# Seven tiles of gathered rows fetched one row at a time by SyncE, in a graph message-passing kernel

## The chip, the cores and the metric

The kernel runs on one core of a Trainium2 chip. The metric is device time in microseconds (us) from start to end of one execution; lower is better. Engines are called PE (TensorE), DVE (VectorE), ACT (ScalarE), POOL (GpSimd) and SP (SyncE). SP only issues DMA transfers.

## The reference

The inputs are 6,250 nodes with 96 features, and 106,250 edges sorted by destination, each with 96 features of its own.

```python
h = jnp.maximum(_layernorm(x, axis=-1), 0.0)
ea = edge_attr @ W_edge.T + b_edge
msg = jax.nn.relu(h[src] + ea)                       # one row per edge
aggr = jax.ops.segment_sum(msg, dst, num_segments=6250)
z = (1.0 + eps) * h + aggr
out = x + jax.nn.relu(z @ W1.T + b1) @ W2.T + b2
```

## The kernel before

**Stages.** First h = relu(layernorm(x)) is computed and stored in DRAM as `h_table`. Then the edges are handled in tiles of 128 edges. There are 830 tiles and a tail of 10 edges, and the tiles are grouped in 43 batches: forty of 20 tiles, then batches of 16, 10 and 4. At the end a two-layer MLP runs over ten blocks of nodes.

**A batch of 20 tiles.** SP loads the transposed edge features with four transfers (`load_edges`, L320). POOL gathers the 128 source rows of each tile from `h_table` with one indirect DMA per tile (`gather`, L375), so a batch costs POOL 20 such instructions; the row numbers are in `src_all`, one column for each tile. PE multiplies the edge features by `w_edge` (L505; it writes them by feature). ACT moves 32x32 blocks out of PSUM (`move_blocks`, L451). DVE transposes them back (L926) and adds the gathered rows in two instructions of ten tiles each (`add_rows`, L941). ACT and DVE split the sum in three bf16 parts (L458, L920, L463, L955). PE sums the parts by destination with a one-hot matrix (L567, L604), which DVE adds up (L853, L825) before it makes the next one-hot matrix (L771).

**What sets the order.** Each engine has a list of its own, and semaphores tie the lists. `edge_in` and `gathered` have two buffers each (`SLOTS = 2`).

- POOL starts the gathers of batch c when PE has begun the edge product of batch c-1 (`edge_begun`) and DVE has added batch c-2 (`added`).
- SP starts the loads of batch c when PE has finished the edge product of batch c-2 (`edge_done`). In batches 17 to 26 it also issues two transfers that fetch x again (L356).
- ACT moves the blocks of batch c when `edge_done` counts c+1.
- On PE the sums of batch c-1 (`agg_done`) stand ahead of the edge product of batch c+1.
- On DVE the adds of batch c stand ahead of the sums of batch c-1.

Of the kernel before, what the change touches and what calls it, by code (L numbers as in the profile page):

```python
# [7 lines left out]
ALU = mybir.AluOpType  # L8
# [8 lines left out]
SIDES = 2  # L17
# [4 lines left out]
BANK = 512  # L22
LN_EPS = 1e-5
LAST_SIDES = (8, 5, 2)
SLOTS = 2
NODE_PARTS = 125
NODE_RUN = 5
# [28 lines left out]
    return [SIDE_TILES] * (rest // (SIDES * SIDE_TILES)) + list(LAST_SIDES)  # L56


def gnn_layer(nc, x, edge_t, src_tiles, dst_tiles, dst_rows, w_edge_t, b_edge,
              eps, w1_t, b1, w2_t, b2, out):  # L60
    N, D = x.shape
    E = edge_t.shape[1]
# [16 lines left out]
    def used_by(c, p, ring):  # L79

        return next((b for b in range(c - ring, -1, -ring) if p < len(pairs[b])), None)

    gathers_to = [[sum(groups[b][g][1] - groups[b][g][0] for b in range(c % SLOTS, c + 1, SLOTS) if g < len(groups[b]))
                   for g in range(len(groups[c]))] for c in range(BATCHES)]
    loads_to = [[sum(g < len(groups[b]) for b in range(c % SLOTS, c + 1, SLOTS)) for g in range(len(groups[c]))]
                for c in range(BATCHES)]
# [29 lines left out]
    with ExitStack() as ctx:  # L116
        def sb(name, shape, dt=F32):
            return ctx.enter_context(nc.sbuf_tensor(name, shape, dt))
# [41 lines left out]
        edge_blocks = sb("edge_blocks", [128, MOST * D])  # L160
        edge_tail_in = sb("edge_tail_in", [D + 1, TAIL])
        tail_gathered = sb("tail_gathered", [TAIL, D])

        dst_by_row = sb("dst_by_row", [BOUND_ROWS, dst_rows.shape[1]], I32)

# [35 lines left out]
        edges_in = [[sem(f"edges_in{b}{g}") for g in range(GROUPS)] for b in range(SLOTS)]  # L201
        gather_in = [[sem(f"gather_in{b}{g}") for g in range(GROUPS)] for b in range(SLOTS)]
        tail_in = sem("tail_in")
        tail_gather_in = sem("tail_gather_in")
        tail_edge_done = sem("tail_edge_done")
        tail_added = sem("tail_added")
# [66 lines left out]
        def flat_rows(rows, k0, k1):  # L273
            if k1 - k0 == PAIR_TILES:
                return rows[:, k0 * D:k1 * D].rearrange("e (h c) -> e h c", h=2)
            return rows[:, k0 * D:k1 * D]

        def in_rows(rows, k0, k1):
            if k1 - k0 == PAIR_TILES:
                return rows[:, k0 * D:k1 * D].rearrange("e (h t d) -> e h t d", h=2, d=D)  # L280
            return rows[:, k0 * D:k1 * D].rearrange("e (t d) -> e t d", d=D)
# [27 lines left out]
        @block.sync  # L309
        def _(sp):  # L310
            sp.dma_start(src_all[:, 0:tiles_of[0]], src_tiles[:, 0:tiles_of[0]]).then_inc(src_first_in, 16)
            for c in range(LN_CHUNKS):
                for a, b in spread:
                    sp.dma_start(x_all[a:b, chunk_of(c)], x_dram[a:b, chunk_of(c)]).then_inc(x_in[c], 16)
            sp.dma_start(w_edge[0:D, :], w_edge_t).then_inc(weights_in, 16)
            sp.dma_start(w_edge[D:D + 1, :], b_edge.rearrange("(a d) -> a d", a=1)).then_inc(weights_in, 16)

            def load_edges(c):
                for g, (k0, k1) in enumerate(groups[c]):
                    sp.dma_start(edge_in[c % SLOTS][0:D, k0 * EDGE_TILE:k1 * EDGE_TILE],  # L320
                                 edges_of(c, k0, k1 - k0)).then_inc(edges_in[c % SLOTS][g], 16)
# [12 lines left out]
            sp.dma_start(src_all[:, tiles_of[0]:TILES + 1], src_tiles[:, tiles_of[0]:TILES + 1]).then_inc(src_rest_in, 16)  # L334
            for c in range(1, len(TABLE_PARTS)):
                if c != ACT_PARTS - 1:
                    store_table(c)
            sp.wait_ge(table_stored, 16 * len(spread) * len(TABLE_PARTS))
            sp.dma_start(dst_by_row[:], dst_rows).then_inc(dst_rows_in, 16)
            sp.dma_start(dst_all[:], dst_tiles).then_inc(dst_in, 16)  # L340
            sp.dma_start(edge_tail_in[0:D, :], edge_t[:, TILES * EDGE_TILE:E]).then_inc(tail_in, 16)
            load_edges(1)
            sp.dma_start(scale_eps[:], eps.rearrange("(a b) -> a b", a=1).broadcast_to((D, 1))).then_inc(late_weights_in, 16)
            sp.dma_start(w1[:], w1_t).then_inc(late_weights_in, 16)
            sp.dma_start(b1_col[:], b1.rearrange("(d a) -> d a", a=1)).then_inc(late_weights_in, 16)
            sp.dma_start(w2[0:D, 0:D], w2_t).then_inc(late_weights_in, 16)
            sp.dma_start(w2[D:D + 1, 0:D], b2.rearrange("(a d) -> a d", a=1)).then_inc(late_weights_in, 16)

            for c in range(SLOTS, BATCHES):
                sp.wait_ge(edge_done, c - SLOTS + 1)  # L350
                load_edges(c)
                if X_FROM <= c < X_FROM + BLOCKS:
                    sp.wait_ge(table_stored, 16 * len(spread) * len(TABLE_PARTS))
                    sp.wait_ge(base_put, BASES)
                    for a, b in spread:
                        sp.dma_start(x_blocks[a:b, c - X_FROM, :], x_by_block[a:b, c - X_FROM, :]).then_inc(x_again_in, 16)  # L356

            for c in range(BLOCKS):
                sp.wait_ge(result_done, c + 1)
                for a, b in spread:  # L360
                    sp.dma_start(out_dram[a:b, c, :], x_blocks[a:b, c, :]).then_inc(stored, 16)
            sp.wait_ge(stored, 16 * BLOCKS * len(spread))

        @block.gpsimd
        def _(pool):
            nc.gpsimd.memset(ident[:], 0.0).then_inc(ident_made, 1)
            pool.wait_ge(ident_made, 1)
            nc.gpsimd.affine_select(out=ident[:], in_=ident[:], compare_op=ALU.not_equal, fill=1.0, base=0,
                                    pattern=[[-1, 128]], channel_multiplier=1).then_inc(ident_made, 1)
            nc.gpsimd.iota(iota_sb[:], [[1, WINDOW]], base=0, channel_multiplier=0,  # L370
                           allow_small_or_imprecise_dtypes=True).then_inc(iota_made, 1)
            def gather(table, c, k):
                at = k * D
                tile = first_tile[c] + k
                nc.gpsimd.indirect_dma_start(  # L375
                    out=gathered[c % SLOTS][:, at:at + D], out_offset=None, in_=table,
                    in_offset=bass.IndirectOffsetOnAxis(ap=src_all[:, tile:tile + 1], axis=0),
                ).then_inc(gather_in[c % SLOTS][k // GROUP_TILES], 16)

            pool.wait_ge(src_first_in, 16)  # L380
            for k in range(FIRST_BURST):
                gather(x, 0, k)
            pool.wait_ge(norm_ready, len(LN_PARTS))
            for k in range(FIRST_BURST, tiles_of[0]):
                gather(x, 0, k)
            pool.wait_ge(src_rest_in, 16)
            pool.wait_ge(table_stored, 16 * len(spread) * len(TABLE_PARTS))
            nc.gpsimd.indirect_dma_start(
                out=tail_gathered[:], out_offset=None, in_=h_table,
                in_offset=bass.IndirectOffsetOnAxis(ap=src_all[0:TAIL, TILES:TILES + 1], axis=0),  # L390
            ).then_inc(tail_gather_in, 16)
            for c in range(1, BATCHES):
                if c >= SLOTS:
                    pool.wait_ge(edge_begun, c)
                for p, (k0, k1) in enumerate(pairs[c]):
                    last_use = used_by(c, p, SLOTS)
                    if last_use is not None:
                        pool.wait_ge(added, adds_to[last_use] + p + 1)
                    for k in range(k0, k1):
                        gather(h_table, c, k)  # L400

        @block.scalar
# [269 lines left out]
        def _(dve):  # L672
# [256 lines left out]
            def add_rows(c):  # L929
                slot = c % SLOTS  # L930
                if by_feature(c):
                    dve.wait_ge(edges_turned, turned_to[c + 1])
                else:
                    dve.wait_ge(edge_done, c + 1)
                for p, (k0, k1) in enumerate(pairs[c]):
                    for g, (g0, g1) in enumerate(groups[c]):
                        if k0 <= g0 < k1:
                            dve.wait_ge(gather_in[slot][g], 16 * gathers_to[c][g])
                    for a, b in pieces(c, k0, k1):
                        put = in_banks(c, a, b) if c < LATE else in_rows(gathered[slot], a, b)  # L940
                        last = nc.vector.tensor_tensor(put, in_banks(c, a, b), in_rows(gathered[slot], a, b), ALU.add)  # L941
                    last.then_inc(added, 1)

            def take_high(c):
# [98 lines left out]
```

## Time and profile before

| | us |
|---|---|
| median of 3 runs | 1229.39 (1229.15 to 1229.55) |
| the profiled execution | 1224.89 |
| span in that execution, first to last instruction | 1223.1 |
| POOL busy | 785.8 |
| DVE busy | 607.6 |
| ACT busy | 518.7 |
| PE busy | 496.0 |

The span is the time between the first and the last instruction; 1.8 us of the profiled execution lie around it. Busy time counts the instructions of an engine and leaves out waits, register work and the issuing of DMAs by SP. An engine that is busy for much less than the span can still set the pace, if its instructions stand apart for a fixed time.

### The profile page before, as it was taken

How to read it: one execution, taken by the hardware profiler on the slowest of the kernel's cores; microseconds unless marked ns; L12 is line 12 of the kernel's file. 1: busy time of each engine (PE TensorE's matmuls, PEld its weight loads, DVE VectorE, ACT ScalarE, POOL GpSimd, SP SyncE). 2: the span in 40 equal slices, each digit the busy share in tenths (PEclk: the TensorE clock that was granted, in tenths of full speed). 3: DMA queues.
4: the chain of work that ended last, by engine and by line, in shares of the span. 5: the costliest groups of instructions: out<-in, count | busy, mean ns of one | idle time of the engine just before them, and what ended most of it. 6: DMA issues, size and time to landing. Idle time of an engine off the chain costs nothing.

```text
span 1223.1 us, 7306 instructions
## 1 busy us (share of the span) xinstructions
PE 496.0 (41%) x1592; PEld 249.7 (20%) x1592; DVE 607.6 (50%) x739; ACT 518.7 (42%) x713; POOL 785.8 (64%) x838
## 2 busy tenths in 40 slices
PE   2143344344344334245343253442534334425358
PEld 2011111222121112012111121120211111112146
DVE  6665544555554445364536345352545363543563
ACT  5134444344433335353435333343535343433434
POOL 6766666666666666575757575766757575757530
PEclk9967766767767766566666665666656666666669
DMA  7523333222223223242323332322423232322212
GB/s 217 148 66 71 83 78 68 67 68 68 67 67 68 68 68 98 56 112 71 81 71 80 72 79 64 72 68 61 101 54 82 63 72 64 71 64 67 47 28 79
DMA packets 51178, 93.18 MB, mean 76 GB/s; under 512 B 17722, under 2 KB 20443, under 8 KB 51136
## 3 DMA queue, kind: packets, MB, share of 16 engines
q0 software_dynamic: 26592, 40.85, 16.1%
q1 hardware_dynamic: 24390, 51.63, 15.6%
q8 instruction: 14, 0.23, 0.1%
q10 hardware_dynamic: 154, 0.24, 0.1%
q14 instruction: 28, 0.23, 0.1%
HBM read 87.85 MB, written 4.80 MB: 76 GB/s over the span
## 4 chain that ended last, share of the span: by engine, by line
another core or an unknown queue 32%; ACT 23%; issue 21%; DVE 13%; PE 6%; DVEq 4%; DMA 1%; SPq 0%; ACTq 0%
ACT edge_blocks L451 17%; ACT msg_parts L458 3%; DVE turn_ps L941 3%; DVE turn_ps L920 3%; PE turn_ps L505 2%; DVEq L834 2%; DVE turn_ps L926 2%; ACT msg_parts L463 2%; DVE msg_parts L955 1%; PE agg_ps L604 1%; PE turn_ps L667 1%; DVEq L836 1%; DVE stats L705 1%; DVE acc L825 1%
## 5 line engine op out<-in xcount | busy, mean ns | idle before, releaser
L375 POOL DMA_INDIRECT gathered<-h_table,src_all x810 | 764.4, 944 | 382.0 <-issue 237.7
L451 ACT COPY edge_blocks<-turn_ps 32x640 f32<-32x640 f32 (+1 forms) x480 | 325.9, 679 | 475.9 <-remote 358.8
L505 PE MATMUL turn_ps<-edge_in,w_edge 97*96 97x512 f32 x398 | 268.2, 842 | 324.2 <-issue 258.8
L926 DVE STREAM_TRANSPOSE turn_ps<-edge_blocks 128x960 f32<-128x960 f32 (+1 forms) x81 | 89.7, 1153 | 216.4 <-ACT edge_blocks L451 115.8
L853 DVE TENSOR_REDUCE sums<-agg_ps 128x192 f32<-128x576 f32 x41 | 30.9, 753 | 319.8 <-remote 319.8
L505 PEld LDWEIGHTS turn_ps<-edge_in,w_edge 97*96 97x96 f32 x398 | 88.6, 234 | 482.9 <-issue 482.9
L604 PE MATMUL agg_ps<-msg_parts,select 128*128 128x288 bf16 x816 | 155.6, 367 | 0.0
L458 ACT ACTIVATE msg_parts<-turn_ps 128x960 bf16<-128x960 f32 (+1 forms) x83 | 79.2, 957 | 157.2 <-DVE turn_ps L941 110.3
L771 DVE TENSOR_TENSOR select<-const_ps,dst_rel 128x2560 bf16<-128x2560 f32 (+1 forms) x43 | 120.8, 2812 | 33.2 <-issue 28.5
L604 PEld LDWEIGHTS agg_ps<-msg_parts,select 128*128 128x128 bf16 x816 | 103.4, 127 | 46.1
L941 DVE TENSOR_TENSOR turn_ps<-turn_ps,gathered 128x960 f32<-128x960 f32 (+1 forms) x83 | 91.1, 1144 | 2.1 <-DVE gathered L760 0.5
L920 DVE SCALAR_TENSOR_TENSOR turn_ps<-turn_ps,msg_parts 128x960 f32<-128x960 f32 (+1 forms) x83 | 91.1, 1144 | 0.3 <-ACT msg_parts L458 0.3
L955 DVE TENSOR_TENSOR msg_parts<-turn_ps,msg_parts 128x960 bf16<-128x960 f32 (+1 forms) x83 | 90.8, 1136 | 0.3 <-ACT msg_parts L463 0.3
L552 PE MATMUL turn_ps<-ident,h_all 125*96 125x125 f32 x50 | 13.1, 415 | 188.4 <-ACT edge_blocks L451 179.9
L567 PE MATMUL agg_ps<-ident,sums 128*96 128x128 f32 x84 | 23.6, 378 | 150.5 <-DVE acc L825 133.9
L463 ACT CAST msg_parts<-turn_ps 128x960 bf16<-128x960 f32 (+1 forms) x83 | 78.2, 945 | 11.6 <-issue 6.6
L552 PEld LDWEIGHTS turn_ps<-ident,h_all 125*96 125x96 f32 x50 | 7.9, 187 | 199.3 <-issue 199.2
L567 PEld LDWEIGHTS agg_ps<-ident,sums 128*96 128x96 f32 x84 | 10.3, 162 | 174.4 <-issue 171.7
L375 POOL DMA_INDIRECT gathered<-x_dram,src_all x20 | 19.6, 981 | 10.9 <-issue 5.5
L526 PE MATMUL turn_ps<-w_edge,edge_in 97*128 97x96 f32 x68 | 14.4, 406 | 27.1 <-DMA edge_in<-edge_t_dram 14.9
L825 DVE TENSOR_TENSOR acc<-acc,agg_ps 96x128 f32 x84 | 23.4, 279 | 0.9
L526 PEld LDWEIGHTS turn_ps<-w_edge,edge_in 97*128 97x128 f32 x68 | 13.9, 315 | 27.3 <-issue 27.3
(77 smaller groups left out, 187.9 us busy)
## 6 DMA issues: line engine op xcount, KB each, us to landing
edge_in<-edge_t_dram SPq DMA_DIRECT2D x165, 240.0 KB
gathered<-h_table,src_all POOLq DMA_INDIRECT x810
x_all<-x_dram SPq DMA_DIRECT2D x5, 420.0 KB
h_all<-x_dram SPq DMA_DIRECT2D x10, 210.0 KB
out_dram<-h_all SPq DMA_DIRECT2D x10, 210.0 KB
h_table<-h_all SPq DMA_DIRECT2D x3, 420.0 KB
h_table<-h_all SPq DMA_DIRECT2D x1, 630.0 KB
dst_by_row<-dst_rows_dram SPq DMA_DIRECT2D x1, 480.0 KB, 4.1
```

What stands on the lines that cost most here:

```text
L375: nc.gpsimd.indirect_dma_start(out=gathered[c % SLOTS][:, at:at + D], out_offset=None, in_=table, in_offset=bass.IndirectOffsetOnAxis(ap=s ...
L451: last = nc.scalar.copy(blocks[e:e + TURN, :, f:f + TURN], edges[f:f + TURN, :, e:e + TURN])
L458: last = nc.scalar.activation(in_parts(msg_parts[c % 2], a, b, 0), in_banks(c, a, b), ACT.Relu)
L463: last = nc.scalar.copy(in_parts(msg_parts[c % 2], a, b, 1), in_banks(c, a, b))
L505: mm = pe.matmul(turn_ps[0:D, q * BANK:q * BANK + (k1 - k0) * EDGE_TILE], w_edge[:], edge_in[c % SLOTS][:, k0 * EDGE_TILE:k1 * EDGE_TILE], ...
L604: mm = pe.matmul(agg_ps[:, s * BANK:s * BANK + SPLIT * D], select[c % 2][:, tile, :], msg_parts[c % 2][:, tile, :, :], start=(t == 0), sto ...
L771: nc.vector.tensor_tensor(select[b][:, 0:tiles, :], iota_ps.unsqueeze(1).broadcast_to((128, tiles, WINDOW)), dst_rel[:, bass.ds(at, tiles) ...
L825: return nc.vector.tensor_tensor(acc[:, cols], acc[:, cols], turned, ALU.add)
L920: return nc.vector.scalar_tensor_tensor(message, message, 0.0, high, ALU.max, ALU.subtract)
L926: last = nc.vector.transpose(in_flat(c, a, b), flat_rows(edge_blocks, a, b))
L941: last = nc.vector.tensor_tensor(put, in_banks(c, a, b), in_rows(gathered[slot], a, b), ALU.add)
L955: last = nc.vector.tensor_tensor(in_parts(msg_parts[c % 2], a, b, 2), in_banks(c, a, b), in_parts(msg_parts[c % 2], a, b, 1), ALU.subtract)
```

## The change

In seven of the forty large batches (6, 11, 16, 21, 26, 31 and 36) POOL gathers 19 tiles and leaves out the last. The 128 rows of that tile are fetched by SP, with one transfer of one row (384 bytes) each, into a buffer of their own (`row_tile`, two of them). The row numbers lie in one partition (`row_index`). SP loads up to 16 of them in registers with one load, and takes the address of each transfer in `h_table` from a register. The 128 transfers of a tile are spread over five batches (25 or 26 in each), after the edge loads of that batch in SP's list: batches 2 to 6 for the first tile, and so on, up to batch 36. Ahead of the first rows of the third and each later tile, SP waits for the adds of the batch that last used the same buffer. DVE adds the second ten tiles of such a batch in three instructions (five tiles, four tiles, and the last tile after a wait for its 128 transfers).

```diff
+ROW_STEPS = 5
+ROW_SLOTS = 2
+PICK = 16
+def row_plan(tiles):
+    plan = batch_plan(tiles)
+    full = plan.index(LAST_SIDES[0])
+    return list(range(SLOTS + ROW_STEPS - 1, full, ROW_STEPS))
...
+    POOL_TILES = [n - (c in row_tile_of) for c, n in enumerate(tiles_of)]
...
+            sp.dma_start(row_index[:], row_src).then_inc(row_index_in, 16)
+            picked = [sp.alloc_register(f"sp_row{i}") for i in range(PICK)]
+            def load_rows(c):
+                j, step = divmod(c - SLOTS, ROW_STEPS)
+                if j >= ROWED:
+                    return
+                if c == SLOTS:
+                    sp.wait_ge(row_index_in, 16)
+                if step == 0 and j >= ROW_SLOTS:
+                    sp.wait_ge(added, adds_to[rowed[j - ROW_SLOTS] + 1])
+                k0, k1 = (EDGE_TILE * n // ROW_STEPS for n in (step, step + 1))
+                for k in range(k0, k1):
+                    if (k - k0) % PICK == 0:
+                        count = min(PICK, k1 - k)
+                        at = j * EDGE_TILE + k
+                        sp.load(picked[0:count], row_index[0:1, at:at + count])
+                    node = sp.snap(picked[(k - k0) % PICK], min_val=0, max_val=N - 1)
+                    sp.dma_start(row_tile[j % ROW_SLOTS][k:k + 1, :],
+                                 h_table[bass.ds(node, 1), :]).then_inc(rows_in[j % ROW_SLOTS], 16)
             for c in range(SLOTS, BATCHES):
                 sp.wait_ge(edge_done, c - SLOTS + 1)
                 load_edges(c)
...
+                load_rows(c)
...
-                    for k in range(k0, k1):
+                    for k in range(k0, min(k1, POOL_TILES[c])):
                         gather(h_table, c, k)
...
+                    if k1 > POOL_TILES[c]:
+                        j = row_tile_of[c]
+                        in_bank = groups[c][-1][0]
+                        for a, b in ((k0, in_bank), (in_bank, POOL_TILES[c])):
+                            nc.vector.tensor_tensor(in_part(c, a, b), in_part(c, a, b), gathered[slot][:, a * D:b * D], ALU.add)
+                        dve.wait_ge(rows_in[j % ROW_SLOTS], 16 * EDGE_TILE * (j // ROW_SLOTS + 1))
+                        own = in_part(c, POOL_TILES[c], k1)
+                        last = nc.vector.tensor_tensor(own, own, row_tile[j % ROW_SLOTS][:], ALU.add)
+                    else:
+                        for a, b in pieces(c, k0, k1):
...
```

## Rows read from the trace of the kernel before

**Rows 1.** The page, busy time of each engine with its share of the span.

```profile
PE 496.0 (41%) x1592; PEld 249.7 (20%) x1592; DVE 607.6 (50%) x739; ACT 518.7 (42%) x713; POOL 785.8 (64%) x838
```

**Rows 2.** Table of waits: total us, times, longest.

```profile
ACT edge_blocks L451 <- remote: 358.8, 25, 17.7
...
POOL gathered L375 <- remote: 138.0, 26, 6.9
```

**Rows 3.** The page, groups by cost: busy us, mean ns, idle before and what ended it.

```profile
L375 POOL DMA_INDIRECT gathered<-h_table,src_all x810 | 764.4, 944 | 382.0 <-issue 237.7
```

**Rows 4.** Timeline of POOL, 404 to 434 us: start, us, instruction, idle before.

```profile
404.68 0.94 POOL L375 DMA_INDIRECT gathered<-h_table,src_all  x1 [3.75 <-remote]
...
428.40 0.94 POOL L375 DMA_INDIRECT gathered<-h_table,src_all  x1 [0.30 <-issue]
433.02 0.94 POOL L375 DMA_INDIRECT gathered<-h_table,src_all  x1 [3.69 <-remote]
```

**Rows 5.** Timeline of POOL, 742 to 802 us.

```profile
743.97 0.94 POOL L375 DMA_INDIRECT gathered<-h_table,src_all  x1 [6.88 <-remote]
...
792.64 0.95 POOL L375 DMA_INDIRECT gathered<-h_table,src_all  x1 [0.30 <-issue]
800.47 0.94 POOL L375 DMA_INDIRECT gathered<-h_table,src_all  x1 [6.88 <-remote]
```

**Rows 6.** Timeline of all engines, stretch 760 to 801 us.

```profile
768.12 8.31 ACT L451 COPY edge_blocks<-turn_ps 32x640 f32<-32x640 f32 x12 [8.24 <-PE turn_ps L505]
...
778.75 2.23 DVE L941 TENSOR_TENSOR turn_ps<-turn_ps,gathered 128x960 f32<-128x960 f32 x2
...
783.14 2.22 DVE L955 TENSOR_TENSOR msg_parts<-turn_ps,msg_parts 128x960 bf16<-128x960 f32 x2
...
784.44 7.74 PE L505 MATMUL turn_ps<-edge_in,w_edge 97*96 97x512 f32 x10 [13.69 <-issue]
...
800.19 0.76 DVE L853 TENSOR_REDUCE sums<-agg_ps 128x192 f32<-128x576 f32 x1 [14.83 <-remote]
```

**Rows 7.** Busy time by window: PE, PEld, DVE, ACT, POOL, PEclk, DMA share, GB/s.

```profile
431.00:432.60 1.60, 0.00 (x0) 0.00 (x0) 0.00 (x0) 0.00 (x0) 0.00 (x0) 0.50 0.00 0
```

**Rows 8.** Timeline of POOL, first gathers after four other stops.

```profile
517.92 0.94 POOL L375 DMA_INDIRECT gathered<-h_table,src_all  x1 [6.86 <-remote]
...
574.47 0.94 POOL L375 DMA_INDIRECT gathered<-h_table,src_all  x1 [6.94 <-remote]
...
1139.46 0.94 POOL L375 DMA_INDIRECT gathered<-h_table,src_all  x1 [6.88 <-remote]
...
1177.03 0.94 POOL L375 DMA_INDIRECT gathered<-h_table,src_all  x1 [5.40 <-PE turn_ps L526]
```

**Rows 9.** Instructions of L356: count, shortest/median/longest ns, first and last start.

```profile
L356 SPq DMA_DIRECT2D h_all<-x_dram x20: 8/402/708, 463.1 to 715.6; - x20
```

**Rows 10.** Timeline of SP, first 40 us and one batch at 461 us.

```profile
5.84 0.28 SPq L316 DMA_DIRECT2D w_edge<-b_edge_dram  x1
6.17 1.80 SPq L320 DMA_DIRECT2D edge_in<-edge_t_dram  x4
...
14.39 0.76 SPq L334 DMA_DIRECT2D src_all<-src_tiles_dram  x1
...
461.28 1.72 SPq L320 DMA_DIRECT2D edge_in<-edge_t_dram  x4
```

**Rows 11.** Register work on DVE (L834, L866, L828): shortest/median/longest ns.

```profile
L834 DVEq TENSOR_LOAD <-bounds_i x86: 298/303/547, 71.3 to 1183.5; - x86
...
L866 DVEq FUSED_REGOPS  x39: 62/63/70, 93.9 to 1158.4; - x39
...
L828 DVEq FUSED_REGOPS  x86: 231/254/268, 93.1 to 1194.7; - x86
```

**Rows 12.** The page, DMA queues: packets, MB, share of 16 engines.

```profile
q0 software_dynamic: 26592, 40.85, 16.1%
```

**Rows 13.** Groups by shape, DVE: busy us, mean ns, idle before.

```profile
L941 DVE TENSOR_TENSOR turn_ps<-turn_ps,gathered 128x960 f32<-128x960 f32 x81 | 90.4, 1161 | 2.1 <-DVE gathered L760 0.5
```

More of the change, by code:

```diff
@@ L56, in batch_plan, with gnn_layer @@
     return [SIDE_TILES] * (rest // (SIDES * SIDE_TILES)) + list(LAST_SIDES)
-def gnn_layer(nc, x, edge_t, src_tiles, dst_tiles, dst_rows, w_edge_t, b_edge,
+def row_plan(tiles):
+    plan = batch_plan(tiles)
+    full = plan.index(LAST_SIDES[0])
+    return list(range(SLOTS + ROW_STEPS - 1, full, ROW_STEPS))
+def gnn_layer(nc, x, edge_t, src_tiles, row_src, dst_tiles, dst_rows, w_edge_t, b_edge,
               eps, w1_t, b1, w2_t, b2, out):
@@ L81, in used_by @@
         return next((b for b in range(c - ring, -1, -ring) if p < len(pairs[b])), None)
-    gathers_to = [[sum(groups[b][g][1] - groups[b][g][0] for b in range(c % SLOTS, c + 1, SLOTS) if g < len(groups[b]))
+    rowed = row_plan(TILES)
+    ROWED = len(rowed)
+    row_tile_of = {c: j for j, c in enumerate(rowed)}
+    POOL_TILES = [n - (c in row_tile_of) for c, n in enumerate(tiles_of)]
+    gathers_to = [[sum(min(groups[b][g][1], POOL_TILES[b]) - groups[b][g][0]
+                       for b in range(c % SLOTS, c + 1, SLOTS) if g < len(groups[b]))
                    for g in range(len(groups[c]))] for c in range(BATCHES)]
@@ L162, in gnn_layer @@
         tail_gathered = sb("tail_gathered", [TAIL, D])
+        row_index = sb("row_index", [1, ROWED * EDGE_TILE], I32)
+        row_tile = [sb(f"row_tile{b}", [EDGE_TILE, D]) for b in range(ROW_SLOTS)]
         dst_by_row = sb("dst_by_row", [BOUND_ROWS, dst_rows.shape[1]], I32)
@@ L203, in gnn_layer @@
         tail_in = sem("tail_in")
+        row_index_in = sem("row_index_in")
+        rows_in = [sem(f"rows_in{b}") for b in range(ROW_SLOTS)]
         tail_gather_in = sem("tail_gather_in")
@@ L276, in flat_rows, with in_part @@
             return rows[:, k0 * D:k1 * D]
+        def in_part(c, k0, k1):
+            g = k0 // GROUP_TILES
+            at = k0 % GROUP_TILES * D
+            return edge_bank(c, g)[:, at:at + (k1 - k0) * D]
         def in_rows(rows, k0, k1):
@@ L938, in add_rows @@
                             dve.wait_ge(gather_in[slot][g], 16 * gathers_to[c][g])
-                    for a, b in pieces(c, k0, k1):
-                        put = in_banks(c, a, b) if c < LATE else in_rows(gathered[slot], a, b)
-                        last = nc.vector.tensor_tensor(put, in_banks(c, a, b), in_rows(gathered[slot], a, b), ALU.add)
+                    if k1 > POOL_TILES[c]:
[8 more added lines that the diff above has]
+                        for a, b in pieces(c, k0, k1):
+                            put = in_banks(c, a, b) if c < LATE else in_rows(gathered[slot], a, b)
+                            last = nc.vector.tensor_tensor(put, in_banks(c, a, b), in_rows(gathered[slot], a, b), ALU.add)
                     last.then_inc(added, 1)
@@ L1013, in by_tile, with by_row @@
         return np.pad(index, (0, tiles * EDGE_TILE - E)).reshape(tiles, EDGE_TILE).T
+    def by_row(index):
+        plan_of = [SIDES * m for m in plan]
+        tiles = [sum(plan_of[:c + 1]) - 1 for c in row_plan(E // EDGE_TILE)]
+        return np.concatenate([index[t * EDGE_TILE:(t + 1) * EDGE_TILE] for t in tiles]).reshape(1, -1)
     def by_side(index):
@@ L1022 @@
         "src_tiles": by_tile(src),
+        "row_src": by_row(src),
         "dst_tiles": by_tile(dst),
```

## The prediction

> **What bounds the kernel now.** I read the page first: no engine is busy for more than 64% of the span, and POOL is the one with 64% [rows 1]. So the question is not which engine is full but who waits for whom. The table of waits says that ACT stood 358.8 us at its block moves and POOL 138.0 us at its gathers, both put down to "remote", a releaser that the profile doesn't know [rows 2]. The groups by cost show that POOL's 810 gathers took 764.4 us, with 237.7 us more in small gaps where nothing was awaited [rows 3]: a gather is 0.94 us and stands 1.25 us from the next.
>
> The timeline of POOL shows how these go together. From about 100 to 490 us POOL runs 20 gathers, stops, and runs 20 more. Such a run starts at 404.68, its last gather at 428.40 (19 steps of 1.248 us), and the next run starts at 433.02: 28.34 us for 20 gathers [rows 4]. After 517 us the runs have 40 gathers: 743.97 to 800.47, 56.50 us [rows 5]. The stop is not a constant: POOL stands 3.69 us after 20 gathers and 6.88 after 40. The difference of the two runs is 28.16 us for 20 gathers, **1.408 us for one**, and only 0.18 us is left over that doesn't grow with the count. So the stop behaves like a backlog of 0.16 us per gather that has to be worked off before PE's signals get through.
>
> Is it really POOL's side, and not the chain of PE, ACT and DVE? One turn of the chain is seen from 768.12: block moves 8.31 us, DVE's adds at 778.75, the last split ends at 785.36, and PE's edge product ends at 784.44 + 7.74 = 792.18 [rows 6]. That is 24.1 us, and the turn before it was released at once. Then DVE, which waits for PE's sums, stands 14.83 us until 800.19, although PE's last recorded product ended 8.0 us earlier. In the shorter runs the same hole shows no instruction on any engine and no DMA at all [rows 7]. What holds PE's signals there I can't name from the profile. But its length goes with the number of gathers in three kinds of run, and two turns of the chain need 48.2 us where the pair takes 56.5. I take it that the middle part, from 40 to 1177 us, costs 1.408 us per gather and hides some 4 us per batch of everything else.
>
> **The change, part by part.** *POOL.* Seven gathers go, one in each of seven batches: 7 x 1.408 = **9.9 us less**. If only the visible step counts, it is 7 x 1.248 = 8.7; if the pace were the chain's, 0. The last run before the end has 26 gathers and takes 37.57 us, 1139.46 to 1177.03 [rows 8], 0.8 more than 28.34 + 6 x 1.408 = 36.8, so the rate holds to 2% there too. I take 1.408. The Trainium skill (Perfetto Trace Analysis, on GPSIMD instructions) says that a GpSimd span is to be timed by start-to-start spacing, not by its duration. By that rule alone the sum would be 8.7 us; the stops say 9.9.
>
> *Does SP's extra traffic load the same hidden thing?* Only a look at other extra transfers can tell. In ten batches SP issues two more transfers (L356, 463.1 to 715.6 us) [rows 9]. The pair of batches from 517.92 to 574.47 has them and takes 56.55 us [rows 8]; the pair from 743.97 has none and takes 56.50. Four more transfers for 0.05 us: 0.01 us each at most. There are 896 row transfers, so that bound is wide: 0 to 11 us back. Four large transfers carried much more data than 51 single rows, so I take 0 and keep 11.
>
> *SP.* A batch gets 25.6 rows on average. One transfer of one row of 384 bytes stands in the trace: it starts at 5.84 and the next at 6.17, 0.33 us. Its address is fixed; the slowest single issue near it took 0.76 (L334) [rows 10]. The register work of a row is not in the trace for SP. On DVE a fused register step takes 0.063 us (one bounded value) to 0.254 (a handful of operations), and a register load 0.303 [rows 11]. So a row costs 0.33 + 0.06 = 0.4 at least and 0.8 + 0.25 + 0.3 = 1.35 at most; I take 0.33 + 0.25 = 0.6, nearest to the like-sized transfer. Per batch that is 25.6 x 0.6 = 15.4, two loads 0.7, and the four edge loads 1.7: 17.8 us. SP has 27 to 28 us per batch and otherwise sleeps, so nothing is late: the next `edge_done` finds it free. The point at which it would not is (27.5 - 2.4) / 25.6 = 0.98 us per row. SP's own new wait (for `added` of a batch five or more back) is long met when SP gets to it. The load of `row_index` is one issue of about 0.4 us at the start, before a stretch in which SP waits.
>
> *DVE.* One add of 1.161 us becomes three shorter ones [rows 13]. Three cost at most 3 x 1.161, 2.3 us more, hidden in the 4 us that the chain has spare per batch; more likely 0.3. Without that cover it would be 2 us over seven batches. The wait for the rows: the last fifth is issued after `edge_done` of two batches earlier, some 50 us before the add, so it passes.
>
> *Gathers themselves.* All row transfers may end up on few DMA engines. The Trainium skill (DMA: Bandwidth & Descriptors, on why a DMA increments its semaphore by 16) says that a one-row transfer runs on one engine, the lowest-numbered. Worked out from the trace: POOL's queue moved 26592 packets in 16.1% of 16 engines' span, 0.118 us per packet [rows 12]. If 26 rows a batch sit on one engine at twice that, it is 6 us of 28. Gathers land at least 7 us before their add (a run's half ends at 768.9, its rows are added at 778.75 or later), so this is hidden.
>
> **Sum.** On the profiled execution 1224.89 - 9.9 = 1215.0. The median of the runs is 4.5 above that execution, so **1219.5**.
>
> **Rivals.**
>
> 1. *The rows load what holds PE's signals* (chance 0.13). For it: that thing is unnamed, and 896 more transfers are many beside 830 gathers. Against: L356 left no trace. At 0.006 us per row half the gain goes (1224.5); at 0.011 all of it (1229.4).
> 2. *SP becomes the bound* (0.19, slower). The mechanism: issuing a row with a register address takes over 0.98 us; then SP's list for a batch outlasts POOL's 27.5 us, edge loads come later each time, and all 35 batches run at SP's pace. At 1.0 us per row this is 28.0 against 28.2, no change yet; at 1.1 it is 30.6, +2.4 x 35 = +84, so 1313; at 1.35 some 37, over 1500. For it: no row shows a register address on SP. Against: the plain issue costs a third of the limit.
> 3. *The pace is the chain's* (0.08). Then nothing changes: 1229.4. For it: the stops are ended by PE. Against: a stop twice as long after twice the gathers, and the 24.1 us turn.
> 4. *Rows crowd one DMA engine* (0.05, slower). It decides if a row holds its engine for over 0.8 us, since 25.6 of them then fill 20 us or more of a batch and gathers come later than the 7 us that they have. If each of the seven stretches of five batches loses 3 us by it, that is 21 - 9.9 = 11 more: about 1240.
>
> The forecast has 0.55: 1217 to 1222. A measurement of this kernel can tell about 0.2%, 2.5 us. Faster by more: forecast and the upper half of rival 1, 0.62. The same: the rest of rival 1, rival 3, a little of rival 2, 0.14. Slower: 0.24. The range reaches from 1217 to 1240; only an SP-bound run lies far above.
>
> **What would show it.** POOL: 803 gathers at 1.25 us spacing, and stops 1.4 us earlier in each run with a rowed batch (55.1 us for 39). SP: rows 0.4 to 0.8 us apart, and edge loads still right after `edge_done`. Wrong would be: edge loads that follow a row without a wait and runs stretched to SP's list (rival 2); unchanged run lengths of 28.3 and 56.5 (rival 3); longer stops after equally many gathers (rival 1); DVE waiting at L941 (rival 4).

## The result and the profile after

| | us |
|---|---|
| before, median of 4 runs beside it | 1229.47 (1229.15 to 1229.75) |
| after, median of 4 runs | 1467.18 (1465.09 to 1469.67) |
| ratio, 95% interval | 1.1934 (1.1913 to 1.1956) |
| after, the profiled execution and its span | 1468.46, 1466.7 |

The change costs 238 us. The forecast was 1219.5. Ratios here and below are of the undisturbed executions; the medians also include single executions that ran 2 to 15% longer than their fellows (1153.97 in e2, 1251.86 in g4, 1238.71 in the kernel before beside f1 to f3).

The page of the changed kernel gives the first answer in its busy times and in the chain that ended last. The columns of the first line are those of [rows 1].

```profile
PE 480.5 (33%) x1592; PEld 241.9 (16%) x1592; DVE 608.9 (42%) x753; ACT 518.9 (35%) x713; POOL 780.4 (53%) x831
...
SPq 52%; issue 39%; DVE 3%; PE 3%; ACT 2%; DMA 1%; DVEq 1%; ACTq 0%
SPq L391 28%; SPq L390 11%; SPq L389 7%; SPq L344 4%; ACT edge_blocks L497 1%; PE turn_ps L713 1%; DVE turn_ps L966 1%; DVE stats L751 1%; SPq L401 1%; PE turn_ps L551 0%; PE turn_ps L659 0%; DVEq L880 0%; PE agg_ps L696 0%; DMA h_table<-h_all 0%; ACT h_all L464 0%
```

No engine does notably more work than in [rows 1] (DVE 608.9 us against 607.6). Half of the chain is SP's own queue: the row transfers (L391), the register step ahead of each (L390), the register loads (L389) and the edge loads (L344). In the kernel before SP's queue was 0% of that chain. "Issue" (39%) stands between SP's instructions too, as the batch shown below will tell.

The table of waits of the changed kernel (total us, times, longest) shows what hangs on it.

```profile
PEld turn_ps L551 <- DMA edge_in<-edge_t_dram: 562.4, 67, 31.4
PE turn_ps L551 <- DMA edge_in<-edge_t_dram: 529.0, 25, 31.1
...
POOL gathered L421 <- PE turn_ps L551: 369.5, 33, 17.4
...
DVE turn_ps L992 <- DMA row_tile<-h_table: 106.6, 7, 18.7
```

PE waits 529.0 us for edge features, which SP loads. POOL then waits for PE's edge product (369.5 us; in [rows 2] its longest wait was 138.0 us, for a releaser the profile doesn't know), and DVE waits once in each of the seven batches for the row tile, 106.6 us in all.

The timeline of SP shows that its list is what fills a batch (start, us from the first to the last of the group, count).

```profile
99.34 1.73 SPq L344 DMA_DIRECT2D edge_in<-edge_t_dram  x4
...
524.26 1.73 SPq L344 DMA_DIRECT2D edge_in<-edge_t_dram  x4
527.41 30.16 SPq L391 DMA_DIRECT2D row_tile<-h_table  x26
557.62 1.73 SPq L344 DMA_DIRECT2D edge_in<-edge_t_dram  x4
...
1275.90 1.73 SPq L344 DMA_DIRECT2D edge_in<-edge_t_dram  x4
```

The 26 rows end at 557.57 and the next edge loads start at 557.62: SP never sleeps between 99 and 1312 us. From 99.34 to 1275.90 there are 33 batches, 35.7 us each, against 28.3 in [rows 4, 5].

How that comes to 238 us is read from PE, whose edge products of batches 3 and 36 start here (the kernel before first, then the changed one).

```profile
108.90 4.50 PE L505 MATMUL turn_ps<-edge_in,w_edge 97*96 97x512 f32 x10 [2.57 <-issue]
...
1042.65 6.64 PE L505 MATMUL turn_ps<-edge_in,w_edge 97*96 97x512 f32 x10 [9.55 <-issue]
```

```profile
114.79 4.50 PE L551 MATMUL turn_ps<-edge_in,w_edge 97*96 97x512 f32 x10 [2.76 <-issue]
...
1278.87 7.36 PE L551 MATMUL turn_ps<-edge_in,w_edge 97*96 97x512 f32 x10 [23.70 <-DMA edge_in<-edge_t_dram]
```

The 33 batches take 1164.1 us instead of 933.8: 230.3 more, 7.0 each. With 5.9 us ahead of batch 3 and 7.4 behind the start of batch 36 this is 243.6, the difference of the two profiled spans (1466.7 and 1223.1). In the kernel before the loads of batch 36 were issued at 993.7, 49 us ahead of the product that needs them; in the changed kernel at 1275.90, 3 us ahead.

Why do 26 rows take 30 us? The instructions of SP in two stretches of this one batch tell it. The first three lines are 527 to 540 us, the other three 540 to 556 (shortest/median/longest ns).

```profile
L390 SPq FUSED_REGOPS  x19: 3/44/712, 527.3 to 539.6; - x19
L391 SPq MOVE row_tile<-h_table x18: 3/29/29, 527.3 to 538.2; - x18
L391 SPq DMA_DIRECT2D row_tile<-h_table x18: 3/228/699, 527.4 to 538.2; - x18
...
L390 SPq FUSED_REGOPS  x5: 13/700/725, 539.6 to 553.7; - x5
L391 SPq MOVE row_tile<-h_table x5: 12/701/719, 540.3 to 555.1; - x5
L391 SPq DMA_DIRECT2D row_tile<-h_table x5: 697/710/1402, 540.3 to 555.8; - x5
```

In the first stretch 18 rows go out, 13 of them up to 532.9: 44 ns for the register step, 29 ns for a move and 228 ns for the transfer, 0.42 us from row to row.

```profile
L391 SPq DMA_DIRECT2D row_tile<-h_table x13: 148/228/406, 527.4 to 532.5; - x13
```

In the 16 us from 540 five rows go out. Each of the three instructions takes about 0.70 us there, even the 29 ns move, and there are gaps of 0.70 us between them as well, so that the rows stand 2.8 to 4.9 us apart. The last three rows, from 556.5, are fast again. The timeline of POOL and of DVE in the same stretch shows when this ends.

```profile
552.06 0.94 POOL L421 DMA_INDIRECT gathered<-h_table,src_all  x1 [0.30 <-issue]
562.98 0.94 POOL L421 DMA_INDIRECT gathered<-h_table,src_all  x1 [9.98 <-PE turn_ps L551]
```

```profile
556.57 0.76 DVE L899 TENSOR_REDUCE sums<-agg_ps 128x192 f32<-128x576 f32 x1 [4.32 <-remote]
```

POOL's gathers run from 529.58 to 553.0. At 556.57 DVE gets PE's signal, and SP's last slow instruction ends at 556.47. In the kernel before the stops end in the same way, with the signal to DVE (800.19 in [rows 6]) and POOL's next gather right behind it (800.47 in [rows 5]). I take it that what holds PE's signals in the kernel before is what slows SP's instructions in this one; the two times 0.1 us apart are the evidence, and no run shows the thing itself.

### The profile page after: what moved, and what is told of

It is laid out like the page before. It is cut to its first block, busy times and chain, and to the rows that moved or that the text cites. A ratio compares the mean times of both kernels' runs of the same rounds, so it can differ in the third digit from the quotient of the medians.

```text
span 1466.7 us, 10074 instructions
## 1 busy us (share of the span) xinstructions
PE 480.5 (33%) x1592; PEld 241.9 (16%) x1592; DVE 608.9 (42%) x753; ACT 518.9 (35%) x713; POOL 780.4 (53%) x831
## 4 chain that ended last, share of the span: by engine, by line
SPq 52%; issue 39%; DVE 3%; PE 3%; ACT 2%; DMA 1%; DVEq 1%; ACTq 0%
SPq L391 28%; SPq L390 11%; SPq L389 7%; SPq L344 4%; ACT edge_blocks L497 1%; PE turn_ps L713 1%; DVE turn_ps L966 1%; DVE stats L751 1%; SPq L401 1%; PE turn_ps L551 0%; PE turn_ps L659 0%; DVEq L880 0%; PE agg_ps L696 0%; DMA h_table<-h_all 0%; ACT h_all L464 0%
## 5 line engine op out<-in xcount | busy, mean ns | idle before, releaser
L421 POOL DMA_INDIRECT gathered<-h_table,src_all x803 | 759.0, 945 | 630.8 <-PE turn_ps L551 369.5
L551 PE MATMUL turn_ps<-edge_in,w_edge 97*96 97x512 f32 x398 | 283.8, 884 | 781.3 <-DMA edge_in<-edge_t_dram 529.0
L551 PEld LDWEIGHTS turn_ps<-edge_in,w_edge 97*96 97x96 f32 x398 | 93.1, 246 | 950.1 <-DMA edge_in<-edge_t_dram 562.4
L650 PE MATMUL agg_ps<-msg_parts,select 128*128 128x288 bf16 x816 | 128.9, 323 | 0.0
L650 PEld LDWEIGHTS agg_ps<-msg_parts,select 128*128 128x128 bf16 x816 | 90.8, 111 | 31.1
L996 DVE TENSOR_TENSOR turn_ps<-turn_ps,gathered 128x960 f32<-128x960 f32 (+1 forms) x76 | 83.7, 1143 | 2.0 <-DVE gathered L806 0.5
L598 PE MATMUL turn_ps<-ident,h_all 125*96 125x125 f32 x50 | 13.1, 415 | 116.2 <-ACT edge_blocks L497 65.2
L992 DVE TENSOR_TENSOR turn_ps<-turn_ps,row_tile 128x96 f32<-128x96 f32 x7 | 1.9, 266 | 106.6 <-DMA row_tile<-h_table 106.6
L613 PE MATMUL agg_ps<-ident,sums 128*96 128x128 f32 x84 | 20.1, 329 | 25.0 <-DVE acc L852 20.4
```

Of the source, the lines that this page charges most:

```text
L421: nc.gpsimd.indirect_dma_start(out=gathered[c % SLOTS][:, at:at + D], out_offset=None, in_=table, in_offset=bass.IndirectOffsetOnAxis(ap=s ...
L551: mm = pe.matmul(turn_ps[0:D, q * BANK:q * BANK + (k1 - k0) * EDGE_TILE], w_edge[:], edge_in[c % SLOTS][:, k0 * EDGE_TILE:k1 * EDGE_TILE], ...
L650: mm = pe.matmul(agg_ps[:, s * BANK:s * BANK + SPLIT * D], select[c % 2][:, tile, :], msg_parts[c % 2][:, tile, :, :], start=(t == 0), sto ...
```

## The experiments

The experiments gave two kinds of result, and without that no number below can be understood: in some groups of runs the kernel before takes about 1224 us and the traces have POOL's stops, in others it takes about 1080 and the traces have none. I write **S** for a chip with stops and **N** for one without. S were chips 4 (e5 to e7) and 11 (g), N were chips 2 (e1 to e4), 14 (f), 8 (h) and 3 (i). Each chip served one group of runs, so the record does not show whether the kind belongs to the chip or to something else that changed between groups. The clock does not make the difference: in the kernel before the mean granted clock was 0.67 to 0.69 on S and 0.69 to 0.71 on N. Every comparison is with the kernel before on the same chip. The first measurement (1229 us) is of kind S. Two theories stood: **A**, SP's list of instructions is longer than a batch, and **B**, the row transfers themselves slow the gathers or PE's signals.

**e1_pool_only.** POOL's part alone.

```diff
-                load_rows(c)
...
-                        dve.wait_ge(rows_in[j % ROW_SLOTS], 16 * EDGE_TILE * (j // ROW_SLOTS + 1))
...
+            for rows in row_tile:
+                nc.vector.memset(rows[:], 0.0)
```

> POOL's part alone: seven gathers fewer, no row is fetched, and DVE adds a tile of zeros for the seven tiles, without a wait (so these tiles' messages lack their source rows). If a gather costs 1.41 us with its share of the stops, 1219.5 us; if only its visible step of 1.25 us, 1220.7; if the chain of PE, ACT and DVE sets the pace, 1229.4. The loss of the changed kernel should be gone in every theory that puts it on SP or on the rows.

Kind N: 1071.33 against 1080.0, ratio 0.9922 (0.9907 to 0.9937), 8.7 us less = 7 x 1.24. The visible step of a gather counts there, and nothing more.

**e2_rows_only.** SP's part alone.

```diff
-                    for k in range(k0, min(k1, POOL_TILES[c])):
+                    for k in range(k0, k1):
```

> SP's part alone: all 896 rows are fetched and waited for, and POOL gathers all 20 tiles in every batch (the rows still come from the row tile). Theory A, SP's list of instructions is the bound: the changed kernel's 1467 us, give or take 15, since POOL's seven gathers are not on the path. Theory B, the row transfers slow down the gathers or PE's signals themselves: 1467 + 10 = 1477.

Kind N: 1081.29 against 1080.0, ratio 1.0009 (0.9999 to 1.0019). 896 rows by SP cost nothing that can be told from no change. Neither theory's number came, as both started from the loss of kind S.

**e3_ten_steps.** The rows of a tile over ten batches, three tiles.

```diff
-ROW_STEPS = 5
+ROW_STEPS = 10
```

> The same rows spread over ten batches each: three tiles, 12 or 13 rows per batch. Theory A, SP's list is the bound: 13 rows take one register load of about 2.8 us and 13 x 0.42 us, 10 us with the edge loads, which SP has behind it before its instructions slow down; SP waits for PE again and the time is 1229.4 - 3 x 1.41 = 1225.2. Theory B, each row transfer costs the rest a fixed time ((1467 - 1219.5) / 896 = 0.28 us): 384 rows give 1225.2 + 106 = 1331.

Kind N: 1075.73 against 1080.0, ratio 0.9965 (0.9953 to 0.9977), 4.3 us less. Three steps of 1.25 us are 3.7.

**e4_fixed_address.** The transfers without register work.

```diff
-                        sp.load(picked[0:count], row_index[0:1, at:at + count])
-                    node = sp.snap(picked[(k - k0) % PICK], min_val=0, max_val=N - 1)
+                    node = (j * EDGE_TILE + k) * 6 % N
...
-                                 h_table[bass.ds(node, 1), :]).then_inc(rows_in[j % ROW_SLOTS], 16)
+                                 h_table[node:node + 1, :]).then_inc(rows_in[j % ROW_SLOTS], 16)
```

> All 896 row transfers at addresses known when the program is built, so SP issues one instruction per row and not three, and loads no registers (the rows fetched are other nodes' rows). Theory A, the count of SP instructions at 0.70 us each is what overruns the batch: at most 26 x 0.7 + 1.7 = 20 us per batch, under POOL's 27, so about 1219.5. Theory B, the transfers themselves cost the time: 1467.

Kind N: 1072.16 against 1080.0, ratio 0.993 (0.9915 to 0.9945), like e1. On this kind it tells nothing about A and B. The four runs together show that there neither the rows nor the register work cost anything that can be told from no change, and POOL has no stops: in each of the four traces its gathers from `h_table` follow one another to the last, less than 1.9 us from start to start.

**e5_change_again.** The changed kernel, unaltered.

> The changed kernel itself, unaltered, beside the kernel before on the chip of these runs. The four runs so far had the kernel before at 1080 us and not at 1229, with no stops of POOL and every transfer's landing in the trace. Theory A in its new form: the stops and SP's slow instructions are one thing that belongs to the chip (or to its recording) of the first measurement; where it is missing the change gives 7 x 1.25 = 8.7 us, 1071. If it comes back here: 1229 before and 1467 after. Theory B, the change is slow by itself: some 240 us over the kernel before on this chip too, near 1320.

This chip was of kind S: 1446.42 against 1224.44, ratio 1.1821 (1.1794 to 1.1849). The loss comes back with the stops.

**e6_registers_only.** Meant as the register work without transfers.

```diff
-                    sp.dma_start(row_tile[j % ROW_SLOTS][k:k + 1, :],
-                                 h_table[bass.ds(node, 1), :]).then_inc(rows_in[j % ROW_SLOTS], 16)
+                    sp.reg_mov(kept, node)
...
```

> SP loads the 896 row numbers into registers and makes an address value of each, and issues no row transfer; a tile of zeros is added (the seven tiles lack their source rows). POOL as in the changed kernel. On a chip without the stops: 1071, like POOL's part alone. On a chip with them: SP has 2 short instructions per row and not 3 and no transfer; if it is the number of instructions that slows SP, the time falls to two thirds of the loss (some 1380); if it is the transfers, to 1219.5.

Kind S: 1215.09 against 1224.44, ratio 0.9924 (0.9909 to 0.9939), 9.4 us less. But the program has 7322 instructions, where the changed kernel has 10074: the register work, whose results nobody used, was removed when the kernel was compiled. So it says nothing on registers. It is POOL's part alone on kind S, and it gives 9.4 us for seven gathers; the forecast of this term was 9.9. The interval of the ratio, 7.5 to 11.1 us, would hold 8.7 as well. POOL's timeline decides: a run of 39 gathers starts here, then one of 40, then the next one of 39.

```profile
459.32 0.94 POOL L421 DMA_INDIRECT gathered<-h_table,src_all  x1 [3.82 <-remote]
...
514.41 0.94 POOL L421 DMA_INDIRECT gathered<-h_table,src_all  x1 [6.70 <-remote]
...
570.92 0.94 POOL L421 DMA_INDIRECT gathered<-h_table,src_all  x1 [6.88 <-remote]
```

The 39 take 55.09 us and the 40 take 56.51, and 55.1 for 39 was the prediction's sign. A gather costs 1.41 us there, stop included.

**e7_four_steps.** Nine tiles, each over four batches.

```diff
-ROW_STEPS = 5
+ROW_STEPS = 4
```

> Nine tiles by SP, each spread over four batches, so 32 rows per batch. On a chip without the stops SP needs 1.7 + 32 x (0.42 + 0.22) = 22 us of a batch of 25, so it still waits for PE, and the time is 1080 - 9 x 1.25 = 1068.8. On a chip with the stops SP's list is longer still: (32 / 25.6) times the changed kernel's 34.8 us per batch, 43 us in 36 batches, near 1750.

Kind S: 1529.19 against 1224.44, ratio 1.2482 (1.2465 to 1.2499). More rows per batch, more loss, but much less than in proportion to SP's list (1750 was expected). A reason may be that POOL stands idle for a longer part of each batch, so that more rows go out at the fast rate; no run tests it.

**f1_fixed_address** and **f2_ten_steps** (kernels as e4 and e3), and **f3_half_rows**, the kernel before with gathers of half the rows:

```diff
-                    out=gathered[c % SLOTS][:, at:at + D], out_offset=None, in_=table,
-                    in_offset=bass.IndirectOffsetOnAxis(ap=src_all[:, tile:tile + 1], axis=0),
+                    out=gathered[c % SLOTS][0:64, at:at + D], out_offset=None, in_=table,
+                    in_offset=bass.IndirectOffsetOnAxis(ap=src_all[0:64, tile:tile + 1], axis=0),
```

> The same kernel as in the run with fixed addresses before (896 row transfers, one SP instruction each, no register work; other nodes' rows are fetched), in the hope of a chip with the stops, where the kernel before takes 1225 to 1229. There: if three SP instructions per row at 0.70 us each are what overruns the batch, one instruction per row fits (20 us of 27) and the time is near 1219.5; if the row transfers themselves cost the time, it stays near 1450. Without the stops: 1072 again.

> Three tiles, 12 or 13 rows per batch, as before, for a chip with the stops. If SP's list is the bound only when it is longer than POOL's batch, 13 rows (10 us at SP's fast rate, at most 13 x 2.1 + 4.5 = 32 us at the slow one, mostly the fast one) leave SP free: 1225 - 3 x 1.41 = 1221. If each row costs a fixed time (0.28 us by the changed kernel), 1221 + 106 = 1327. Without the stops: 1075.7 again.

> The kernel before with gathers of 64 rows each (the first 64 edges of each tile; the other 64 get zeros), and as many gathers as before, no row by SP. It asks what the stops of POOL grow with. If with rows moved, the backlog per gather is half of 1.41 us and under the step, so the stops go, and the time falls to POOL's step times 810 or to the chain's 24 us per batch, 1060 or less. If with the count of gather instructions, the stops stay as they are: 1225. Without the stops on this chip it only gives POOL's step for 64 rows.

All three fell on kind N. f1: 1070.44 against 1080.37, ratio 0.9915 (0.99 to 0.993). f2: 1076.95, ratio 0.997 (0.9959 to 0.9981). f3: 1050.27, ratio 0.9722 (0.9707 to 0.9736), so that a gather of 64 rows costs nearly as much as one of 128. The profile has 903 ns instead of 944 and the same small gaps.

**g1_change, g2_fixed_address, g3_ten_steps, g4_half_rows.** The same four kernels, and this chip was of kind S (before: 1223.88).

> The changed kernel once more. Chips so far fall in two kinds: on three sets of runs the kernel before took 1224 to 1229 (twice) with stops of POOL, on two others 1080 without. On the first kind the change should give 1446 to 1467 again; on the second, where it has not run yet, 1080 - 8.7 = 1071.

1445.1, ratio 1.1789 (1.1727 to 1.1852). The loss is there for the third time.

> 896 row transfers with one SP instruction each and no register work. Of use on the kind of chip with stops: near 1219 if the count of SP instructions overruns the batch, near 1450 if the transfers do. On the other kind 1071 again.

1237.35, ratio 1.0113 (1.0052 to 1.0175). By e6's ratio POOL's part alone would be 1214.6 on this chip, so 896 transfers with one instruction each cost 23 us (16 to 31 by the interval of the ratio), and the changed kernel's cost 230. So it is not the transfers as such (B), but what SP has to get through for each. SP's table of waits shows that it sleeps again, where the changed kernel's waits at L344 came to 77 us (33 + 44), all of them after its last rows at 1312 us:

```profile
SPq L344 <- remote: 370.2, 24, 27.0
SPq L344 <- PE turn_ps L550: 68.2, 7, 22.5
```

> Three tiles by SP, 13 rows per batch. On the kind of chip with stops: 1221 if SP's list matters only where it is longer than POOL's batch, 1327 if each row costs a fixed time. On the other kind 1076 again.

1243.61, ratio 1.0168 (1.015 to 1.0186). It is between the two expected values: 24 us over the 1219.7 of three gathers fewer. The timeline of SP says why half the rows don't bring half the loss, nor none.

```profile
518.56 9.22 SPq L391 DMA_DIRECT2D row_tile<-h_table  x13
...
533.93 44.40 SPq L391 DMA_DIRECT2D row_tile<-h_table  x13
578.38 1.73 SPq L344 DMA_DIRECT2D edge_in<-edge_t_dram  x4
...
584.20 5.65 SPq L391 DMA_DIRECT2D row_tile<-h_table  x13
...
598.14 20.18 SPq L391 DMA_DIRECT2D row_tile<-h_table  x13
```

Thirteen rows take 5.7 us when they are issued in the fast part, and 44.4 us when they fall in the slow one; the edge loads that stand behind them are then late. The expectation that 13 rows would mostly meet the fast part was wrong.

> Gathers of 64 rows, as many as before, no rows by SP. On the kind of chip with stops: 1060 or less if the backlog grows with the rows or with time, 1225 if it grows with the number of gather instructions. On the other kind 1050 again.

1227.01, ratio 1.0024 (1.0012 to 1.0037). Half the rows, and the time (0.2% more) and the length of a run are as before: timeline of POOL, first gathers after two stops, to be read against [rows 5].

```profile
525.04 0.90 POOL L375 DMA_INDIRECT gathered<-h_table,src_all  x1 [8.38 <-remote]
...
581.52 0.91 POOL L375 DMA_INDIRECT gathered<-h_table,src_all  x1 [8.37 <-remote]
```

A run of 40 gathers takes 56.48 us (56.50 before), although each step is shorter; the stop makes up for it. So on kind S a gather instruction costs 1.41 us with its share of the stop, for 64 rows as for 128.

**h1_change, h2_registers_kept, h3_four_steps.** The change and e7 for kind N, and a kernel whose register work can't be removed:

```diff
-                    sp.dma_start(row_tile[j % ROW_SLOTS][k:k + 1, :],
-                                 h_table[bass.ds(node, 1), :]).then_inc(rows_in[j % ROW_SLOTS], 16)
+                    sp.reg_alu(kept, kept, node, ALU.max)
+                last_node = sp.snap(kept, min_val=0, max_val=N - 1)
+                sp.dma_start(kept_rows[j % ROW_SLOTS][step:step + 1, :],
+                             h_table[bass.ds(last_node, 1), :]).then_inc(rows_in[j % ROW_SLOTS], 16)
...
```

> The changed kernel, still without a time on the kind of chip where the kernel before takes 1080 us: there 1071. On the other kind 1445 again.

Kind N: **1070.96 against 1081.49, ratio 0.9913 (0.9895 to 0.9932)**. There the change is a gain, of 10.5 us. Its instructions of SP are all at the fast price (same columns as above), and its timeline shows SP asleep at the end of a batch:

```profile
L389 SPq TENSOR_LOAD <-row_index x70: 1016/2256/3572, 40.1 to 872.8; - x70
```

```profile
L390 SPq FUSED_REGOPS  x896: 44/44/59, 41.3 to 878.9; - x180
```

```profile
L391 SPq MOVE row_tile<-h_table x896: 29/29/37, 41.4 to 879.0; - x180
L391 SPq DMA_DIRECT2D row_tile<-h_table x896: 224/228/299, 41.5 to 879.1; - x180
```

```profile
488.99 1.73 SPq L344 DMA_DIRECT2D edge_in<-edge_t_dram  x4
...
495.43 13.17 SPq L391 DMA_DIRECT2D row_tile<-h_table  x26
515.17 1.73 SPq L344 DMA_DIRECT2D edge_in<-edge_t_dram  x4
```

The list of this batch ends at 508.6, 19.6 us after it began, and the next begins at 515.17. The slowest of 896 transfers took 299 ns; on the chip of the first measurement the slowest took 1412.

The same instructions, summed over all rowed batches in the two traces of the changed kernel, tell where the loss of kind S sits:

| SP, us in all | kind N (h1) | kind S (first measurement) |
|---|---|---|
| 70 register loads | 154 | 109 |
| 896 register steps | 40 | 163 |
| 896 moves | 26 | 140 |
| 896 transfers | 208 | 275 |
| gaps behind a step, a move or a transfer, up to the next one of these | 110 | 472 |

The loads do not take longer on kind S. The time is lost in the three short instructions of each row and in the gaps between them.

> SP loads all 896 row numbers into registers and takes the largest of them, and issues one transfer per batch with that address, not 25.6 (a tile of zeros is added for the seven tiles). It has the register loads of the changed kernel, the register steps packed into six per batch, and almost none of the transfers. On the kind of chip with stops: 1215, like POOL's part alone, if the row transfers and the many instructions between them fill SP's list; about 1215 + 35 x 3 = 1320 or more if the register loads (3.5 us for 16) alone were enough. On the other kind 1071.

Kind N: 1070.95, ratio 0.9911 (0.9892 to 0.993), as expected there. **i1_registers_kept** repeated it in the hope of kind S:

> The same kernel as in the run before with the registers kept (row numbers loaded, one transfer per batch). If this chip is of the kind with stops: 1215 if the register loads alone don't overrun SP's batch, 1320 or more if they do. Otherwise 1071 again.

Kind N again: 1074.26 against 1081.84, ratio 0.9924 (0.9908 to 0.9941); its profiled execution took 1084.05 at a granted clock of 0.59, the other four 1069.76 to 1074.67 at 0.70 to 0.71. No run has the loads without the rows on kind S; that they are not the loss is read from the sums above.

> Nine tiles by SP, 32 rows per batch. On the kind of chip without stops 1080 - 9 x 1.25 = 1068.8, a little better than the change, since SP's list of 22 us still fits in a batch of 25. On the other kind 1529 again.

Kind N: 1068.36, ratio 0.9887 (0.9869 to 0.9905), 13.1 us less for nine gathers. It is the fastest version with full gathers on kind N, and the slowest on kind S (e7). Its register loads are all cheap:

```profile
L389 SPq TENSOR_LOAD <-row_index x72: 1152/1227/1402, 40.6 to 894.8; - x72
```

Each of them loads 16 numbers and starts at a multiple of 16 bytes in `row_index`. In h1 only the loads of the first and fourth batch of each five start so: 28 of the 70, 1.0 to 1.4 us each. The other 42 took 3.5 to 3.6 us for 16 numbers and 2.1 to 2.4 for 9 or 10. e3's 30 loads of 12 or 13 numbers divide the same way, 0.9 to 1.3 us and 2.9 to 3.0.

**What tells the kinds apart in a trace.** The list of DMA issues ends with the median time from issue to landing. In the changed kernel's first profile it is missing, in the same kernel on kind N it is there:

```profile
edge_in<-edge_t_dram SPq DMA_DIRECT2D x165, 240.0 KB
```

```profile
edge_in<-edge_t_dram SPq DMA_DIRECT2D x165, 240.0 KB, 3.4
```

It is so in all the profiles: no landing time for these 165 transfers in the nine of kind S (before, after, e5, e6, e7 and g1 to g4), and one of 3.4 to 4.4 us in the profiles of kind N. Kind S loses records of semaphores: for the same 10074 instructions the trace of the changed kernel holds 6830 semaphore events in the first measurement and 19987 in h1. That would fit a recorder that can't keep up and makes the engines wait for it, since it is SP's cheapest instructions that take 0.70 us, and a gather costs 1.41 us, twice that, however little it moves. But every execution that gave a time has a span and a clock on record, so none is known to have run unrecorded; this was not tested, and the cause of the stops and of the slow instructions is not settled.

## Why the prediction was wrong

**The step that failed** is the price of a row on SP: "I take 0.33 + 0.25 = 0.6", from which "nothing is late". On kind N the sum was right: register step, move and transfer are 0.30 us of work and 0.42 us from row to row, and the loads, 22 us for a tile's ten in h1, add 0.17: 0.59 us per row. Part of that is luck, as the register step was taken too long (0.25 us for 0.04) and the loads too short (0.7 us for the two of a batch, where they took 2.2 to 5.9). On the chip of the measurement the same row costs 1.3 us on average, 35.7 us per batch instead of the 17.8 of the forecast for SP's list, because SP's short instructions take 0.70 us for most of a run of gathers.

**Where it should have been seen.** I had found the backlog, could not name it, and asked only whether the rows would lengthen it (rival 1, with L356 as the evidence). I didn't ask what it does to an engine that has many cheap instructions. All prices of SP in [rows 10] stand right after a release or before the first run of gathers. But the answer was in the trace of the kernel before, in the very transfers of [rows 9]: seven of the twenty took 0.69 to 0.71 us, all of them late in a run of 40 gathers. Timeline of SP, with POOL's run from 517.92 to 574.47:

```profile
542.96 1.72 SPq L320 DMA_DIRECT2D edge_in<-edge_t_dram  x4
546.76 2.10 SPq L356 DMA_DIRECT2D h_all<-x_dram  x2
...
576.52 0.81 SPq L356 DMA_DIRECT2D h_all<-x_dram  x2
```

```profile
L356 SPq DMA_DIRECT2D h_all<-x_dram x2: 699/700/700, 546.8 to 548.2; - x2
```

The same two transfers took 0.37 and 0.40 us at 576.52, at the start of a run, and 0.70 each at 546.76, with a gap of 0.70 between them. The four edge loads just ahead, at 542.96, took their usual 0.31 to 0.43 us each, so it is not the place in the run alone that sets the price; what else does is open. I had read the length of the batches that hold these transfers, 0.05 us more, and not the transfers themselves.

**Rival 2 was the right one**, with its mechanism: edge loads come later each time, and the batches run at SP's pace. Its threshold of 0.98 us per row agrees with the runs: at 0.59 us nothing was late (h1), and at 1.3 the batches took 35.7 us. It had a chance of 0.19, and the range left it out. The bound of 1.35 us per row in the paragraph on SP was close to what came, though not for its reason: it put a row at the dearest single issue of the start and a register load of its own (0.8 + 0.25 + 0.3).

**POOL's part was right**, but it showed only where the rows were left out. Seven gathers fewer gave 9.4 us on kind S (e6; 9.9 forecast from the stops, and the runs of 39 gathers 1.4 us shorter as forecast) and 8.7 on kind N, where there are no stops and the visible step of 1.25 us is all. The rule of the Trainium skill (Perfetto Trace Analysis, GPSIMD Engine Instruction) that a GpSimd instruction is timed by its start-to-start spacing is the right price on kind N; on kind S a run's length gives 1.41 us per gather, and the stops belong to it. In the changed kernel on kind S POOL waits for SP's list, and there is no sign of the 9.9 us.

**Rival 3** (the chain's pace) falls with e1 and e6. **Rival 4** (one DMA engine) falls with e2 and h1 on kind N, 896 rows without a loss, and with g2 on kind S, where the same number of transfers cost a tenth of the change's loss. **Rival 1** is true in a small way on kind S: 896 transfers at fixed addresses cost 23 us (g2), 0.025 us each, more than the gain. It would have been enough to turn the sign. How much of it is held signals and how much SP's own slow instructions, g2 does not tell apart.

**DVE.** The three adds and the wait for the rows cost nothing of their own; the 106.6 us of waiting for the row tile come from SP's late rows.

## What to carry to other kernels

When a stop grows with the count of another engine's instructions, treat it as something shared until a run shows otherwise. Before a second engine is given many cheap instructions, read every instruction of that engine that falls late in such a run, one by one and not by the group's median: seven transfers of 0.70 us were there to be read. Where a helper queue takes over work, sum its list per batch with the worst price in the trace. Putting the loads that everything waits for a whole batch ahead of the rows may also help; no run here tried it. And look whether the profile has landing times: where they were missing here, the same change cost 18 to 19% instead of gaining 0.9%, so a second chip is worth a run before such a gain or loss is trusted.

## What the runs showed of the hardware that was not expected

- The same program took 1080 to 1082 us on four chips and 1224 to 1229 on two others and in the first measurement, and the same change is worth -0.9% on the first and +18 to +19% on the second.
- On the second kind an instruction of SP that takes 29 ns (a move) takes 0.70 us while POOL works through a run of gathers: in the batch shown from 3.6 us after the start of the first gather to 3.5 us after the end of the last.
- A gather of 64 rows costs POOL nearly what one of 128 does: 903 and 944 ns on the first kind, and on the second 1.41 us with its share of the stops either way (g4).
- A load of 16 registers on SP took 1.2 us when its first number stood at a multiple of 16 bytes in `row_index`, and 3.5 us otherwise (h1, h3); the load of one register on DVE took 0.30 us [rows 11].
